# Convolution banks, square-based second-norm statistics, one joint root and a later W2 centring in a fused attention and expert kernel

## What is computed

```python
x = x + conv_attention(ln_c(x))        # attention over channels: softmax(q k^T) per head of 8 channels,
                                       # then Wout (attn v) + bout, a 64x64 map applied to all positions
t = tokens(x)                          # 1024 tokens of 64 channels for each image
t2 = ln_t(t)                           # second norm, over the 64 channels of a token
logits = mean(t2, over tokens) @ Wr + br
# softmax, capacity scale, softmax, top 2 experts for each image, softmax of the two weights
out = sum_k w_k * (gelu(t2 @ W1[e_k] + b1[e_k]) @ W2[e_k] + b2[e_k])
t = t + layer_norm(out + t2, gamma, beta)   # third norm
```

## Time and profile before

| | us |
|---|---|
| median of 3 runs | 108.69 (108.67 to 108.73) |
| the profiled execution's own time | 108.59 |
| its span in the profile | 106.8 |
| TensorE busy | 88.7 (83% of the span), 748 matmul records |
| VectorE busy | 70.9 (66%) |
| ScalarE busy | 48.2 (45%) |
| GpSimd busy | 32.2 (30%) |

### The profile page before, as it was taken

One profiled execution on the slowest core, in us unless ns is written; L12 is line 12 of the kernel. 1 busy time (PEld: TensorE's weight loads), 2 busy tenths in 40 slices (PEclk: granted clock), 3 DMA queues, 4 the chain that ended last, 5 costly groups with the idle time before them and its releaser, 6 DMA issues.

```text
span 106.8 us, 2258 instructions
## 1 busy us (share of the span) xinstructions
PE 88.7 (83%) x748; PEld 47.8 (45%) x749; DVE 70.9 (66%) x258; ACT 48.2 (45%) x83; POOL 32.2 (30%) x77
## 2 busy tenths in 40 slices
PE   5967898998999999777976999599999999986200
PEld 1424776997665437355922237133333333242100
DVE  0098999842789978989999943714537256668920
ACT  0000946647321111103747899996795895510000
POOL 5000000005200000004428199956261900861400
PEclk9999999999999999999999999999999999999975
DMA  3899999400000000001420125680000080056065
GB/s 56 302 396 312 269 303 345 84 0 0 0 6 0 0 0 0 3 6 47 101 52 6 32 69 130 153 201 7 6 0 0 0 185 18 0 132 147 15 147 147
DMA packets 6554, 9.82 MB, mean 92 GB/s; under 512 B 1040, under 2 KB 3344, under 8 KB 6544
## 3 DMA queue, kind: packets, MB, share of 16 engines
q1 hardware_dynamic: 4848, 6.77, 24.1%
q10 hardware_dynamic: 1696, 2.92, 9.6%
HBM read 5.49 MB, written 2.10 MB: 71 GB/s over the span
## 4 chain that ended last, share of the span: by engine, by line
PE 58%; DVE 15%; ACTq 9%; ACT 7%; issue 5%; DVEq 1%
PE pC L1188 14%; PE pC L955 5%; ACTq L281 5%; PE pA L906 4%; PE pB L896 3%; PE pA L967 3%; PE pA L1163 3%; ACTq L276 3%; PE pB L1163 3%; PE pM L996 2%; DVE bst L644 2%; ACT SQ L406 2%; PE pC L1180 2%; PE pS L1030 2%; ACT U L290 2%
## 5 line engine op out<-in xcount | busy, mean ns | idle before, releaser
L457 POOL TENSOR_TENSOR LO<-UF,HI 128x512 f16<-128x512 f32 x8 | 9.2, 1157 | 23.5 <-ACT HI L324 22.6
L1188 PE MATMUL pC<-H,w2g 128*64 128x512 f32 x64 | 15.8, 602 | 0.0
L576 DVE BATCH_NORM_STATS2 bst<-XT 128x6 f32<-128x128 f32 x32 | 7.1, 282 | 5.2 <-DMA XT<-x_tok_dram 5.2
L230 POOL TENSOR_TENSOR XT<-XT,T 128x512 f32<-128x512 f32 x6 | 7.5, 1269 | 4.0 <-DVE XT L858 4.0
L1076 PE MATMUL pM<-wz 128*128 128x512 bf16 x25 | 7.1, 444 | 1.3 <-POOL wz L450 1.3
L393 ACT ACTIVATE H<-pA,b1s 128x1024 f32<-128x1024 f32 x6 | 6.7, 1111 | 2.5 <-PE pA L1163 2.3
L473 POOL COPY w1g<-w1hl 128x256 f16 x14 | 5.1, 403 | 8.1 <-issue 6.0
L324 ACT CAST HI<-UF 128x512 f16<-128x512 f32 x8 | 4.8, 619 | 6.0 <-DVE UF L677 6.0
L463 POOL TENSOR_TENSOR w1hl<-SQ,w1hl 128x512 f16<-128x512 f32 x2 | 2.3, 1154 | 17.2 <-DVE A L623 17.2
L644 DVE BATCH_NORM_STATS2 bst<-pA 128x6 f32<-128x128 f32 x32 | 6.9, 284 | 0.6 <-PE pA L967 0.5
L834 DVE TENSOR_SCALAR U<-pC,c,wsm 128x512 f32<-128x512 f32 x8 | 6.2, 801 | 1.4 <-PE pC L1188 0.9
(11 more groups left out here) (219 smaller groups left out, 186.7 us busy)
## 6 DMA issues: line engine op xcount, KB each, us to landing
out_dram<-XT SPq DMA_DIRECT2D x14, 128.0 KB, 2.4
XT<-x_tok_dram SPq DMA_DIRECT2D x2, 512.0 KB, 9.3
X<-x_cha_dram SPq DMA_DIRECT2D x8, 128.0 KB, 11.0
X<-x_cha_dram ACTq DMA_DIRECT2D x8, 128.0 KB, 10.9
ST<-HI SPq DMA_DIRECT2D x6, 128.0 KB, 2.4
ST<-LO SPq DMA_DIRECT2D x6, 128.0 KB, 2.4
XT<-x_tok_dram SPq DMA_DIRECT2D x2, 256.0 KB, 4.8
XT<-x_tok_dram ACTq DMA_DIRECT2D x2, 256.0 KB, 5.1
```

The costliest lines, as they stand in the source:

```text
L230: engine.tensor_tensor(OUT[:, p, cols], V[:, p, cols], T[:, p, cols], ALU.add).then_inc(s_fin[2 * p + h], 1)
L457: nc.gpsimd.tensor_tensor(LO[:, p, cols], UF[:, p, cols], HI[:, p, cols], ALU.subtract).then_inc(s["lo"], 1)
L576: return nc.vector.bn_stats(bst[:, p, j, :], XT[:, p, j * P:(j + 1) * P].rearrange("p (b c) -> p c b", b=2))
L1188: last = mm(half(y_ps[:, b * HALF:(b + 1) * HALF], h), w2g[:, p % 2, b, k, :], H[:, step % 2, b, h * HALF:(h + 1) * HALF], start=False, st ...
```

## The change

Four things are changed.

1. Odd pairs are convolved into other PSUM banks (pS and the second half of pB), even pairs as before into pC, so conv(p) waits for the residual of pair p-2 and no longer of the one before. Both batches of a convolution stand together in the order.
2. For pairs 0 and 1 the statistics of the second norm come from sums of squares. ScalarE squares T into UF (four halves, `square_t`). The matrix wrbd has two more columns that give the sum over the channels times C^-0.5, and a second matrix sqbd sums the squares; `squares(p)` accumulates into the bank of `scores(p)`. After the turning of the scores, ScalarE squares the sums (`square_means`) and VectorE subtracts (`squared_stats`, one instruction of 128x32). `turn_t` and `turned_stats` stay for pairs 2 and 3.
3. The first norm's root of pairs 2 and 3 is one call, after the statistics of both.
4. W2 is centred after the first half of `spread2(0)` and its second half, into pC, and ScalarE copies it after `round_hi(0, 1)`, just before the Gelu table.

The orders of TensorE, ScalarE and VectorE are written anew around these. The diff, cut to its core:

```diff
+        def moments(i):
+            src = small_bank[0][:, 0:HALF].rearrange("p (g r) -> p g r", r=32)
+            return src[:, :, 2 * E + 2 * i:2 * E + 2 * i + 2]
-        ut, cv, tt = pA, pC, pA
+        ut, tt = pA, pA
+        cv = [[pC[:, 0:HALF], pC[:, HALF:N]], [pS[:, :], pB[:, HALF:N]]] * 2
-        ps_w2 = [pM[:, 0:HALF // 2], pB[:, HALF:HALF + HALF // 2]]
+        ps_w2 = [pC[:, 0:HALF // 2], pC[:, HALF:HALF + HALF // 2]]
 # ScalarE
+            def square_means():
+                act.wait_ge(s["sc"], 2)
+                nc.scalar.activation(msq[:, :].rearrange("p (g h) -> p g h", h=2), moments(0),
+                                     ACT.Square).then_inc(s["msq"], 1)
+            def square_t(p, b):
+                act.wait_ge(s["t"], 2 * p + b + 1)
+                cols = slice(b * HALF, (b + 1) * HALF)
+                nc.scalar.activation(UF[:, p, cols], T[:, p, cols], ACT.Square).then_inc(s["sq2"], 1)
-            split_w1(0) evac_gram(0) evac_u(0) split_w1(1) evac_u(1) evac_u(2) softmax_exp(0) evac_gram(1)
-            evac_u(3) evac_b1(0) evac_mt(0) softmax_exp(1) (copies of w2c) evac_b1(1) evac_mt(1)
-            evac_scores(0) to (3) round_hi(0, 0) exp round_hi(0, 1)
+            evac_u(0) evac_gram(0) split_w1(0) evac_u(1) split_w1(1) softmax_exp(0) evac_gram(1) evac_u(2)
+            evac_b1(0) evac_mt(0) softmax_exp(1) evac_u(3) evac_b1(1) square_t(0, 0) evac_mt(1)
+            square_t(0, 1) square_t(1, 0) square_t(1, 1) evac_scores(0) evac_scores(1) square_means()
+            evac_scores(2) evac_scores(3) round_hi(0, 0) exp round_hi(0, 1) (copies of w2c)
 # GpSimd, after the memsets of iota
+            for h in range(2):
+                nc.gpsimd.memset(wrbd[h * C:(h + 1) * C, 2 * E + h:2 * E + h + 1], C ** -0.5).then_inc(s["wrz"], 1)
+                nc.gpsimd.memset(sqbd[h * C:(h + 1) * C, 2 * E + 2 + h:2 * E + 3 + h], 1.0).then_inc(s["wrz"], 1)
+                pool.wait_ge(s["wrz"], 2 * h + 2)
 # VectorE
+            def squared_stats():
+                dve.wait_ge(s["sc"], 2)
+                dve.wait_ge(s["msq"], 1)
+                nc.vector.tensor_tensor(square_sums(bst2, 0, 2), moments(1), msq[:, :].rearrange("p (g h) -> p g h", h=2),
+                                        ALU.subtract).then_inc(s["bt"], 1)
-            token_stats(2) rstd1(2, 1, token_stats(3) between) scale1(2) rstd1(3, 1, att_p1(0) between) scale1(3)
-            att_scores(0) att_probs(0) att_p1(1) att_bias(0) att_scores(1) residual1(0) att_probs(1) residual1(1)
-            turned_stats(0, 0) att_bias(1) turned_stats(0, 1) residual1(2) turned_stats(1, 0) residual1(3)
-            turned_stats(1, 1), (2, 0), (2, 1), (3, 0), (3, 1) rstd2()
+            token_stats(2) token_stats(3) rstd1(2, 2) scale1(2) att_p1(0) scale1(3)
+            att_scores(0) att_probs(0) att_p1(1) att_scores(1) att_bias(0) att_probs(1) residual1(0) residual1(1)
+            att_bias(1) residual1(2) residual1(3)
+            turned_stats(2, 0), (2, 1), (3, 0) squared_stats() turned_stats(3, 1) rstd2()
 # TensorE
             def conv(p, b):
-                if p >= 1:
-                    pe.wait_ge(s["t"], 2 * p + b - 1)
+                if p == 1:
+                    pe.wait_ge(s["cbs"], 1)
+                elif p >= 2:
+                    pe.wait_ge(s["t"], 2 * (p - 2) + b + 1)
             def turn_t(p, b):
-                    pe.wait_ge(s["bt"], 2 * p + b - 1)
+                    pe.wait_ge(s["bt"], b + 1)
+            def squares(p):
+                pe.wait_ge(s["sq2"], 2 * p + 2)
+                for q in range(4):
+                    chunks = UF[:, p, :].rearrange("p (b q n) -> p q b n", b=2, q=4)[:, q]
+                    last = mm(ps_st[32 * q:32 * (q + 1), 0:2 * P].rearrange("p (b n) -> p b n", b=2), sqbd[:, :], chunks,
+                              start=False, stop=True)
+                last.then_inc(s["st"], 1)
-            gram(0) centre_w1() gram(1) transpose_u(0) att_p1(0) transpose_u(1) gram(2) att_s(0) transpose_u(2)
-            gram(3) transpose_u(3) att_b1(0) att_p1(1) att_mt(0) att_s(1) conv(0, 0) conv(0, 1) centre_w2()
-            conv(1, 0) conv(1, 1) att_b1(1) turn_t(0, 0) att_mt(1) turn_t(0, 1) conv(2, 0) conv(2, 1)
-            turn_t(1, 0) scores(0) conv(3, 0) turn_t(1, 1) conv(3, 1) turn_scores(0) scores(1) turn_t(2, 0)
-            turn_t(2, 1) turn_scores(1) scores(2) turn_t(3, 0) turn_t(3, 1) turn_scores(2) scores(3) turn_scores(3)
+            gram(0) transpose_u(0) gram(1) centre_w1() att_p1(0) transpose_u(1) gram(2) att_s(0) gram(3)
+            transpose_u(2) att_p1(1) att_b1(0) att_s(1) att_mt(0) transpose_u(3) conv(0, 0) conv(0, 1) att_b1(1)
+            conv(1, 0) conv(1, 1) att_mt(1) scores(0) conv(2, 0) conv(2, 1) squares(0) conv(3, 0) conv(3, 1)
+            scores(1) turn_t(2, 0) squares(1) turn_t(2, 1) turn_scores(0) turn_t(3, 0) turn_scores(1)
+            turn_t(3, 1) scores(2) turn_scores(2) scores(3) turn_scores(3)
             bias_logits(0) bias_logits(1) spread2(0, 0) logits(0) logits(1) spread2(0, 1)
+            centre_w2()
```

More of the change, by code:

```diff
@@ L126, in build_program @@
         wrbd = sb("wrbd", [P, 32])
+        sqbd = sb("sqbd", [P, 32])
+        msq = sb("msq", [P, 2 * G2])
         SR = sb("SR", [P, 2, 2 * P])
@@ L355, in _ @@
             softmax_exp(1)
-            act.wait_ge(s["w2p"], 1)
-            for h in range(2):
-                nc.scalar.copy(w2c[:, h * HALF // 2:(h + 1) * HALF // 2], ps_w2[h]).then_inc(s["w2v"], 1)
+            evac_u(3)
             evac_b1(1)
+            square_t(0, 0)
             evac_mt(1)
-            for p in range(NP):
-                evac_scores(p)
+            square_t(0, 1)
+            for b in range(2):
+                square_t(1, b)
+            evac_scores(0)
+            evac_scores(1)
+            square_means()
+            evac_scores(2)
+            evac_scores(3)
             round_hi(0, 0)
@@ L1095, in _ @@
             att_s(0)
+            gram(3)
             transpose_u(2)
-            gram(3)
+            att_p1(1)
+            att_b1(0)
+            att_s(1)
+            att_mt(0)
             transpose_u(3)
-            att_b1(0)
-            att_p1(1)
-            att_mt(0)
-            att_s(1)
-            conv(0, 0)
-            conv(0, 1)
-            centre_w2()
-            conv(1, 0)
-            conv(1, 1)
+            for b in range(2):
+                conv(0, b)
             att_b1(1)
-            turn_t(0, 0)
+            for b in range(2):
+                conv(1, b)
             att_mt(1)
-            turn_t(0, 1)
-            conv(2, 0)
-            conv(2, 1)
-            turn_t(1, 0)
             scores(0)
-            conv(3, 0)
-            turn_t(1, 1)
-            conv(3, 1)
-            turn_scores(0)
+            for b in range(2):
+                conv(2, b)
+            squares(0)
+            for b in range(2):
+                conv(3, b)
             scores(1)
             turn_t(2, 0)
+            squares(1)
             turn_t(2, 1)
+            turn_scores(0)
+            turn_t(3, 0)
             turn_scores(1)
+            turn_t(3, 1)
             scores(2)
-            turn_t(3, 0)
-            turn_t(3, 1)
             turn_scores(2)
```

96 lines of the change are left out of this document (45 added, 51 removed).

## The result

The changed kernel takes 103.36 us (median of 4 runs, 103.30 to 103.64) against 108.71 for the kernel before, run beside it: a ratio of 0.9507, interval 0.9483 to 0.9531, so 5.35 us faster. Five more runs gave 103.38 and 0.9516 (0.9503 to 0.9529). I had forecast 104.2 with a range from 103.5 to 105.5. The direction and the mechanism came out; the gain of 4.5 was 0.85 too small, and the range ended 0.14 above the median. The profiled execution took 103.30 us with a span of 101.5, against 108.59 and 106.8.

A forecast was written before the change was run, and what follows sets the result against it. TensorE and VectorE near full, with the spreading matmuls at 46.10 the point to move. 108.59 - 4.7 + 0.2 = 104.1, plus 0.10 to the median: 104.2 us; own range 103.5 to 104.9, to 105.5 with the first rival.

The forecast's parts named there:

- Step 1: First transforms to second norm's roots: work that goes, VectorE 3.4 us of statistics, TensorE 3.2 us net.
- Step 2: Head: old gaps close, first convolution starts at 27.4 instead of 27.82, -0.4 us (ends -0.9 and +0.2).
- The new gap: Head: second pair's scores wait 0.6 us for VectorE's p1s.
- Step 3: First convolution to second norm's root, walked through the queues: root starts at 39.1 against 44.06, -4.96 us.
- Step 4: End of second norm: TensorE, not VectorE's root (done 41.1), sets the spreading, 41.4 against 46.10, -4.7 us.
- Step 5: Router stretch: W2's centring moved later, 0.3 of its 1.1 us uncovered; 0.2 us taken as cost.
- my two ends: W2's centring: cost 0 if the first up-projection's wait hides the 0.3 us, 0.3 if TensorE itself is last.
- the cost is 0: First up-projection: its 0.70 us wait for the expert's index and register load hides the centring's uncovered 0.3 us.
- The rule on tables: ScalarE's new squares: no table load priced; by the skill's 2.66 us per switch the total would be about 108.5.
- TensorE's hand-overs: First convolution onward: about 12 steps on TensorE each cost 0.1 us more, time 105.4; chance 0.17.
- the slower case: Stretch before the router: pauses drop TensorE's clock, half speed in 45 to 60 us, time 113.0; chance 0.04.

The follow-up runs named there:

- the repeated kernel: The changed kernel, unaltered, run once more for its ratio and trace: 103.38 us, ratio 0.9516.
- the best version: Changed kernel with the last pair's scores in their own bank and GpSimd's first subtraction held until VectorE subtracted the router's maximum: 102.04 us.
- the trace whose clock fell in the head: Changed kernel with the second group's B1 matmuls behind both batches of the second convolution: 104.06 us; profiled execution 105.48 us.

## Why the prediction missed its range

**Step 1** held: every count is as forecast and every price within 0.1 us.

**Step 2** (start of the convolution, -0.4) was mis-sized: -0.75 in the first trace, -0.61 and -0.66 between the repeated kernel's 27.16 and the two values of before. The new gap was right (0.65 for 0.6). The step that failed is "TensorE starts the Gram matrix at 11.08". That start depends on when input and constants arrive, and the kernel before could not use an early arrival, because ScalarE held W1's centring; moving the centring and ScalarE's Gram copy gives 0.33 us. The new head puts the convolution 17.09 us behind VectorE's first scaling. For the 10.24 of the trace that I walked from, that is 27.33, and I had forecast 27.4. But 10.24 was a late start: over all 17 traces it lies between 9.97 and 10.38 with a median of 10.08. So the length of the head was right to 0.1 us, and the rest of this miss is an anchor taken from one execution. How far one profiled execution missed by it (0.26) is chance.

**Step 3** had the mechanism and the order right and two sizes wrong, which partly cancel. TensorE needed 13.74 us from the first convolution to the spreading for my 14.0. By the scores of tile 0 it was 0.61 ahead of my walk (2.69 us behind the first convolution for 3.3), since two convolutions with B1 among them took 2.0 us where I had 2.55. From the end of tile 2's scores to the spreading it lost 0.28 again (3.18 for 2.9): the hand-overs between scores, copy and turn are longer than I walked them. That these two leave only -0.26 is luck. VectorE's root came 1.1 us before my time, which did not matter.

**Step 4** was right in what it says: TensorE is the later one, and giving the last scores a bank proves it. The distance is 0.84 us where I had 0.3.

**Step 5** was wrong by its 0.2. Neither removing nor doubling the centring moves the time by what five runs can tell. Tile 1's spreading did come late, by 0.21 us where I had 0.3 (4.15 us behind tile 0's for 3.94 before). What failed is the choice of 0.2 between my two ends: the pause before the first up-projection hid all of it, shrinking from 0.70 to 0.50, and that was my own case of "the cost is 0". Behind it lies a second reserve that I did not see, VectorE's stand-still beside GpSimd (0.53 us for an instruction of 0.17); with that taken out the doubled centring costs 0.39. The two copies before the Gelu table cost nothing either: ScalarE's idle time before the tanh shrank from 1.33 to 0.79 us.

**The rule on tables.** The groups of ScalarE's instructions have two table loads, as before:

```profile
L351 ACT ACT_TABLE_LOAD x1 | 1.3, 1283 | 10.8 <-issue 10.8
L395 ACT ACT_TABLE_LOAD x1 | 1.3, 1283 | 0.0
```

The squares at 624 ns need none of their own. The Trainium skill (ScalarE: Activation LUTs, section Table sets: the hidden batching unit) has the compiler put a load before every activation that needs one. The trace has none at the squares, so they were no change of set, and the 108.5 worked out for such a change did not come. The prediction doesn't show how the 108.5 is made up; two switches of 2.66 us in full on top of 104.2 would be 109.5.

**The rivals.** TensorE's hand-overs do bind, but at the end only and at a lower price than 105.4. The clock was 1.00 in both stretches where a fall was feared, so the slower case has nothing for it:

```profile
27.00:41.00 14.00, 12.96 (x138) 6.16 (x138) 12.09 (x40) 5.52 (x14) 0.00 (x0) 1.00 0.01 2
45.00:60.00 15.00, 13.57 (x132) 7.08 (x132) 11.49 (x59) 11.93 (x18) 8.34 (x18) 1.00 0.22 54
```

TensorE was busy 12.96 of 14.00 us where the pauses were feared.

**The range.** The terms erred in one direction, three times in a row (0.33, 0.26, 0.20). The lower end, 103.5, had 0.5 us of room for the head and 0.2 for the centring and none for the stretch between them, Steps 3 and 4, where 0.26 came. Each miss alone would have stayed within it; the three together did not. The parts are not additive either: taken back one at a time, one pair of banks costs 2.9, turned statistics 2.6 and two roots 0.75, together 6.3 us for a gain of 5.35. So each is worth that much only with the others in place; what it would give alone, on the kernel before, was not run.

## What to carry to other kernels

A walk through the queues with measured durations gave 84% of a gain of 5.35 us. Its errors were a start time taken from one trace, matmuls that overlap and were walked one behind the other, and a delay that a later wait hid. Before a step is called on the path, ask which instruction releases the next one, and whether that instruction took as long as its like elsewhere in the trace; here one that was three times as long as its twin was a hidden wait. When two engines pass a bank back and forth, count the waits of all pairs on both sides and not of the first, and take no start time from one trace for an anchor.

## What the runs showed that I had not expected

VectorE stands still beside GpSimd, and the trace books it as busy time of the instruction that stands: 0.53 for 0.17 us (128x8, one input and two constants), 0.89 for 0.23 (128x64, two inputs out of SBUF). Both are in the trace of before as well, and between them a third, in VectorE's timeline:

```profile
49.01 0.89 DVE L746 TENSOR_TENSOR rout<-rout,rsm 128x64 f32<-128x64 f32 x1
...
51.69 0.72 DVE L756 TENSOR_SCALAR rsm<-rsm 128x8 f32<-128x8 f32 x1
...
56.91 0.54 DVE L790 TENSOR_SCALAR wk<-rsm 128x8 f32<-128x8 f32 x1
```

The one in the middle stands on the router's path and ends with GpSimd's second LO (51.23 + 1.16 = 52.39 against 52.41). No run moved it: it takes 0.71 us in the best version too (at 45.26), for 0.17 of its like, so some 0.5 us may be left there, an estimate from these two. Reductions (0.22) and the multiplication with an input out of PSUM (0.68) ran beside the same GpSimd work at their own price. The Trainium skill (SBUF — State Buffer, section Who interferes with whom) says that the two engines share one pair of SBUF ports, that a `tensor_scalar` can take it and a `tensor_tensor` with two SBUF inputs needs it against GpSimd's reads, while a `tensor_reduce` does not, and that the loser stands for the whole of the other's instruction. The rows agree as far as they reach: both kinds stood still beside LO, the reduction did not, and wk ended with GpSimd's LO. They don't show the ports themselves. I had not looked for it in the trace of before.

The arrival of the first loads moves between executions: VectorE scaled first between 9.97 and 10.38 us, and TensorE's first weight matmul, which waits for the constants, started between 8.41 and 9.55. The changed head passes this on: its convolution stood 17.08 or 17.09 us behind the scaling in nine traces, and 17.33 and 17.34 in the two whose constants came after 9.4 (the trace whose clock fell in the head left out). The kernel before mostly did not: its convolution came at 27.82 and 27.77 for starts of 10.24 and 10.04.

The eight small fp32 B1 matmuls (64x64) run among the pieces of the convolutions at hardly any price: 0.15 and 0.06 us of chain for what takes 0.28 alone.
